# A 64-expert layer on one core: two of four batches as 127 tiles of expert-sorted rows, between two dense parts

## The chip, the cores and the metric
The kernel runs on one core of a Trainium2 chip. The metric is the device time of one execution in microseconds, the median over several runs. TensorE is PE here, its weight loads PEld, VectorE DVE, ScalarE ACT, GpSimd POOL, SyncE SP.

## The reference
A decoder of four rounds over x of 4 batches x 512 tokens x 128 features: each round has an attention, a cross attention and a feed-forward part, each added to x. The change is in the feed-forward part of the third round, a mixture of 64 experts with 8 chosen per token. In short, with h the layernorm of x:
```
logits = h @ gate_w.T                        # 64 per token
p      = softmax(logits); w = top 8 of p, divided by their sum
x     += sum over the 8 of w[e] * (silu(h @ w_gate[e].T) * (h @ w_up[e].T)) @ w_down[e].T
```
`w_gate` and `w_up` are 64 x 96 x 128, `w_down` is 64 x 128 x 96. Everything is float32.

## The kernel before, in words
The program is a row of stages. Each stage is a block in which every engine runs its own list in program order and waits on semaphores that are written out by hand, and a stage ends when all engines are through. x, y and a are resident tensors of 128 features x 2048 tokens; `k.big` holds a layer's weights, loaded by SP well ahead; `k.ps` are the eight PSUM banks of 512 columns. `layer8` (L1764) is the 64-expert layer.

It computes all 64 experts for all tokens. The 64 x 96 hidden features are cut into J = 48 blocks of 128, and a unit is one block for one batch of 512 tokens: units go over pairs of batches, blocks, and the two batches of a pair, 192 in all. A unit is nine matmuls of 128x512 by `three` (L770), which makes a float32 product of three fp32r ones, with the weights split in `wh` + `wl` and the data in `yh` + `yl`: three for the gate, three for up, and, LAG = 3 units later, three for the down product, which add up in `sums` over the 48 blocks. ACT takes the silu of the gate (L1934), DVE (even units, L2023) or POOL (odd ones, L1840) multiplies it by the routing weights, DVE multiplies by up (L2001), ACT copies the result to `hh` (L1940) and DVE takes the rest `hl` (L2006). POOL splits the weights of a block (L1829, L1831). The routing weights come as `rep`: 128 hidden features x 1024 tokens, in which each row repeats its expert's weight. SP reads them in two or three pieces per block from `routing` in DRAM (L1820), into a ring of R = 3.

Before the first unit, DVE finds the top 8 of batches 0 and 1 with `max` and `match_replace`, norms, transposes and stores the weights; those of batches 2 and 3 follow in 12 steps between units (`route`, L1992 is `finish`).

The 8-expert layer of the first round, `layer2` (L778), already works on sorted rows, and rows of it are among those below. There POOL scatters token rows of 512 bytes to the places of their expert in DRAM by indirect DMAs of 128 rows (L906), SP reads back four tiles at a time (L869) and fetches the experts' weights (L861), PE turns the tiles (L938) and multiplies with the expert's columns addressed from registers that it loads in `address`, twice in all (L948, L952, L965), DVE copies results out (L1144), SP stores them (L874), POOL gathers them back (L828) and DVE mixes them with their shares (L844, L846). The places in DRAM are cleared before, by POOL at the start of the program (L169). `l0_lookup_mlp` (L318) is the second half of the first stage's layer, with its last matmuls at L353 and its last add at L424.

## Time and profile before
| | |
|---|---|
| median of 3 runs | 2006.56 us (2006.14 to 2015.05) |
| the profiled execution, its own time | 1991.04 us |
| its span, first to last instruction | 1989.2 us |
| mean granted TensorE clock over the span | 0.938 |
| busy: PE, PEld, DVE, ACT, POOL | 1764.9, 1270.9, 1239.4, 1058.3, 830.7 us |
| DMA: bytes, mean | 131.88 MB, 66 GB/s |

Busy time is that in which an engine worked on an instruction; a matmul's includes its way through the array, so matmuls that follow each other overlap. A line of the page and of the trace names the line of the code, the engine, the operation and the tensors (out<-in, without buffer numbers). "idle before" is the time for which the engine stood still ahead of the group, with what ended it. The clock is a fraction of 2.4 GHz.

### The profile page before, as it was taken

How to read it: one execution, taken by the hardware profiler on the slowest of the kernel's cores; microseconds unless marked ns; L12 is line 12 of the kernel's file. 1: busy time of each engine (PE TensorE's matmuls, PEld its weight loads, DVE VectorE, ACT ScalarE, POOL GpSimd, SP SyncE). 2: the span in 40 equal slices, each digit the busy share in tenths (PEclk: the TensorE clock that was granted, in tenths of full speed). 3: DMA queues.
4: the chain of work that ended last, by engine and by line, in shares of the span. 5: the costliest groups of instructions: out<-in, count | busy, mean ns of one | idle time of the engine just before them, and what ended most of it. 6: DMA issues, size and time to landing. Idle time of an engine off the chain costs nothing. (4 is left out here: it accounts for less than half of the span.)

```text
span 1989.2 us, 50832 instructions
## 1 busy us (share of the span) xinstructions
PE 1764.9 (89%) x20095; PEld 1270.9 (64%) x20114; DVE 1239.4 (62%) x2436; ACT 1058.3 (53%) x2386; POOL 830.7 (42%) x1085
## 2 busy tenths in 40 slices
PE   7883998756899999999998779999999999999886
PEld 4332997334568888888887537888788756633332
DVE  4544444477667777777853437888888768634434
ACT  4551444557776666666644345555555541166552
POOL 1004231124457767676652006666666610044201
PEclk9996999977899999999997889999999989699998
DMA  7002784000230000000000405444444300000100
GB/s 282 1 1 77 216 255 138 14 1 0 74 108 15 24 14 25 14 24 14 17 22 24 191 6 147 129 130 130 127 128 128 106 1 1 1 2 1 39 1 22
DMA packets 51182, 131.88 MB, mean 66 GB/s; under 512 B 11288, under 2 KB 23200, under 8 KB 50048
## 3 DMA queue, kind: packets, MB, share of 16 engines
q1 hardware_dynamic: 47040, 121.24, 19.4%
q0 software_dynamic: 2816, 7.21, 1.1%
q8 instruction: 164, 2.69, 0.6%
q14 instruction: 74, 0.61, 0.1%
q10 hardware_dynamic: 1088, 0.13, 0.0%
HBM read 110.47 MB, written 18.09 MB: 65 GB/s over the span
## 5 line engine op out<-in xcount | busy, mean ns | idle before, releaser
L2558 DVE SCALAR_TENSOR_TENSOR big<-bank,pack,big 128x256 f32<-128x256 f32 (+2 forms) x384 | 182.9, 477 | 39.3 <-ACT mask L2447 23.5
L2006 DVE TENSOR_TENSOR hl<-bank,hh 128x512 fp32r<-128x512 f32 x192 | 132.8, 692 | 65.2 <-ACT hh L1940 55.6
L1940 ACT ACTIVATE hh<-bank 128x512 fp32r<-128x512 f32 x192 | 115.1, 599 | 86.0 <-DVE bank L2001 84.5
L2446 ACT ACTIVATE big<-bank,pack 128x256 f32<-128x256 f32 x192 | 91.5, 477 | 129.0 <-PE bank L2254 124.7
L773 PE MATMUL bank<-yh,wl 128*128 128x512 f32 x384 | 151.6, 395 | 5.4 <-DVE yl L1950 2.5
L774 PE MATMUL bank<-yl,wh 128*128 128x512 f32 x384 | 150.5, 392 | 0.0
L775 PE MATMUL bank<-yh,wh 128*128 128x512 f32 x384 | 150.4, 392 | 0.0
L1840 POOL TENSOR_TENSOR a<-a,rep 128x512 f32<-128x512 f32 x96 | 125.5, 1307 | 30.4 <-DMA rep<-routing 25.7
L2001 DVE TENSOR_TENSOR bank<-bank,a 128x512 f32<-128x512 f32 x192 | 133.2, 694 | 7.0 <-PE bank L775 0.9
L2958 ACT ACTIVATE pt<-bank 128x1024 f32<-128x1024 f32 (+3 forms) x128 | 79.5, 705 | 99.1 <-PE bank L2810 99.0
L2164 POOL TENSOR_TENSOR big<-big,mask 128x256 f32<-128x256 f32 (+1 forms) x128 | 93.8, 732 | 88.8 <-DVE big L2558 56.4
L2740 POOL TENSOR_SCALAR_AFFINE_SELECT pt<-pt 128x256 f32<-128x256 f32 x128 | 55.0, 442 | 175.3 <-ACT pt L2958 173.0
L2254 PE MATMUL bank<-y,pack 128*128 128x262 f32 (+1 forms) x384 | 120.8, 400 | 4.2 <-DVE big L2558 4.0
L2241 PE MATMUL bank<-big 128*128 128x128 f32 x896 | 123.2, 284 | 1.4 <-issue 1.4
L1829 POOL CAST wh<-big 128x384 fp32r<-128x384 f32 x96 | 48.8, 508 | 167.9 <-PE bank L775 114.2
L2241 PEld LDWEIGHTS bank<-big 128*128 128x128 f32 x896 | 107.1, 191 | 6.6 <-issue 3.0
L2984 DVE TENSOR_REDUCE part<-bank 128x8 f32<-128x1024 f32 (+1 forms) x80 | 93.8, 1218 | 24.5 <-PE bank L2790 23.8
L1139 DVE SCALAR_TENSOR_TENSOR a<-bank,big,a 128x128 f32<-128x128 f32 x184 | 51.8, 344 | 83.5 <-ACT a L1051 83.4
L1831 POOL TENSOR_TENSOR wl<-big,wh 128x384 fp32r<-128x384 f32 x96 | 98.7, 1028 | 7.7
L2790 PE MATMUL bank<-big 32*128 32x128 f32 (+1 forms) x1024 | 92.6, 355 | 4.2 <-DVE part L2984 4.2
L2790 PEld LDWEIGHTS bank<-big 32*128 32x128 f32 x1024 | 74.3, 222 | 33.0 <-issue 18.8
L773 PEld LDWEIGHTS bank<-yh,wl 128*128 128x128 f32 x384 | 72.5, 189 | 29.4 <-issue 4.8
(601 smaller groups left out, 4504.8 us busy)
## 6 DMA issues: line engine op xcount, KB each, us to landing
rep<-routing SPq DMA_DIRECT2D x64, 384.0 KB, 3.5
big<-in_experts SPq DMA_DIRECT2D x46, 516.0 KB, 3.8
rep<-routing SPq DMA_DIRECT2D x64, 256.0 KB, 4.0
big<-in_big SPq DMA_DIRECT2D x1, 9216.0 KB, 26.3
gate<-big SPq DMA_DIRECT2D x32, 256.0 KB, 2.0
z<-gate SPq DMA_DIRECT2D x16, 512.0 KB
rep<-routing SPq DMA_DIRECT2D x64, 128.0 KB, 3.7
pack<-in_pack SPq DMA_DIRECT2D x1, 5846.5 KB, 21.1
```

The source lines that it names most:

```text
L773: nc.tensor.matmul(out, pl, dh[:, cur], start=start, stop=False)
L774: nc.tensor.matmul(out, ph, dl[:, cur], start=False, stop=False)
L775: return nc.tensor.matmul(out, ph, dh[:, cur], start=False, stop=stop)
L1831: nc.gpsimd.tensor_tensor(low, src, high.bitcast(F32), ALU.subtract).then_inc(s["w_low"], 1)
L1840: nc.gpsimd.tensor_tensor(spread_(m), spread_(m), spread(n), ALU.mult).then_inc(s["odd"], 1)
L1940: nc.scalar.activation(hh[:, sl((n - 1) % 3)], up_bank(n - 1), ACT.Copy).then_inc(s["high"], 1)
L2001: nc.vector.tensor_tensor(up_bank(n), up_bank(n), other, ALU.mult).then_inc(s["h"], 1)
L2006: nc.vector.tensor_tensor(hl[:, sl(n % 3)], up_bank(n), hh[:, sl(n % 3)].bitcast(F32), ALU.subtract).then_inc(s["low"], 1)
L2241: mm4 = lambda out, gr, left_, right: [nc.tensor.matmul(out[:, sl(h % GH, P)], left_(h), right(h), start=True, stop=True) for h in hs(gr)][-1]
L2254: nc.tensor.matmul(haloed(i)[:, :, 3 - halo:], k.w["L2_attn_qkv_w"][:, sl(m, P)], tokens, start=True, stop=True).then_inc(s["raw"], 1)
L2558: ins = nc.vector.scalar_tensor_tensor(out=d, in0=conv_in(i, back), scalar=weight(i, 3 - back), in1=d, op0=ALU.mult, op1=ALU.add)
L2790: mm = nc.tensor.matmul(both(at)[:, gl * S + c * w:][:, 0:w], qj[b][rows, j * S + i * P:][:, 0:P], kd[b][rows, key:key + w], start=kind != ...
```

## The change
Batches 2 and 3 stay dense, batches 0 and 1 become rows sorted by expert. The layer's list on PE is: blocks 0 to 25 of batches 2 and 3 (52 units), then 127 tiles of 128 rows (8 x 1024 rows and up to 127 rows of padding for each of 64 experts, rounded down), two to a step, then blocks 26 to 47 (44 units).

- In a dense unit gate and up are still three fp32r matmuls each; the down product is one matmul of float32, `h` is no longer split, LAG is 2 and the silu goes to SBUF (`sg`). POOL multiplies and splits weights only for the first five blocks, then DVE multiplies for all units and takes `wl`, ACT makes `wh`. Blocks now cover 4 experts x 32 features, three blocks share a `rep` row set, and SP loads a quarter per expert (4 DMAs per 3 blocks).
- In the first part DVE also ranks the picks of batches 0 and 1 (a scan), finds each row's place (`locate`, `situate`), and for each of the 8 picks writes 8 columns of places (`put`). POOL then issues 64 indirect DMAs (L1901 of the changed kernel) that scatter the rows to `wide_rows`.
- In the tile part SP reads four tiles per DMA and stores the results two tiles at a time, from two places in `out`. PE transposes four tiles at a time (L1969) and then computes, two tiles at a step, gate and up together as one matmul of 192 columns (L1981), a transpose of `h` (L1989), the down matmul (L1996). Every 8 steps it loads 32 addresses into registers (L1974). ACT does `lay`, silu, `tile_lay`; DVE the product and `evict`.
- In the second dense part POOL issues 64 indirect DMAs that gather the results (L1907), 8 per 128 tokens, into two halves of `found`, and DVE mixes 8 rows with their shares after units 60, 64, 69, 73, 78, 82, 87 and 91. PE turns the sums back (`join`) and DVE adds them to x.
- SP clears the 127 tiles' rows in DRAM with six DMAs at the end of `l0_lookup_mlp` (L340 of the changed kernel), and the 8-expert layer's SP waits for them before its first fetch. A second copy of the down weights, 96 x 8192, is loaded in the first dense part (`wide_down`).

```diff
+WIDE_TILES = (2 * S * 8 + 64 * (P - 1)) // P
+WIDE_SPLIT, WIDE_POOLED, WIDE_PLACE_AT, WIDE_MAP_AT = 26, 5, 8, 15
+WIDE_MIX_AT = [2 * WIDE_SPLIT + 8 + 9 * i // 2 for i in range(8)]
...
+        @block.sync
+        def _(sp):
+            sp.wait_ge(s["down"], B)
+            for lo in range(0, WIDE_TILES, SORTED):
+                n = min(SORTED, WIDE_TILES - lo)
+                sp.dma_start(k.wide_rows[lo * P:(lo + n) * P, :].rearrange("(n p) d -> p n d", p=P), k.big[:, 0:n * D].rearrange("p (n d) -> p n d", d=D)).then_inc(k.wide_cleared, 16)
...
+            sp.wait_ge(k.wide_cleared, 16 * -(-WIDE_TILES // SORTED))
...
+        sg, h = (lambda n: k.past[:, sl(n % 2)]), (lambda n: a[:, sl(n % 3)])
...
+            def bring_rows(q):
+                after(sp, s["turned"], q - 2)
+                n = min(4, WIDE_TILES - 4 * q)
+                src = rows_in[4 * q * P:(4 * q + n) * P, :].rearrange("(n p) d -> p n d", p=P)
+                sp.dma_start(rows[:, q % 3 * S:][:, 0:n * P].rearrange("p (n d) -> p n d", d=D), src).then_inc(s[f"x_{q % 3}"], 16)
+
+            def store(p):
+                n = len(tiles(p))
+                sp.wait_ge(s["evicted"], p + 1)
+                dst = rows_out[2 * p * P:(2 * p + n) * P, :].rearrange("(n p) d -> p n d", p=P)
+                sp.dma_start(dst, out[:, p % 2 * 2 * P:][:, 0:n * P].rearrange("p (n d) -> p n d", d=D)).then_inc(s[f"stored_{p % 2}"], 16)
...
+            sp.wait_ge(s["scattered"], 16 * K8 * HALF)
+            bring_rows(0)
+            bring_rows(1)
+            for p in range(PAIRS):
+                if p % 2 == 0 and p // 2 + 2 < turns:
+                    bring_rows(p // 2 + 2)
+                store(p)
+            for q in range(before, G // 4):
+                bring_rep(q)
...
+            for m in range(WIDE_POOLED):
                 n = 2 * m + 1
...
-                nc.gpsimd.tensor_tensor(spread_(m), spread_(m), spread(n), ALU.mult).then_inc(s["odd"], 1)
-                if m + 2 < N // 2:
...
+                nc.gpsimd.tensor_tensor(sg(n), sg(n), spread(n), ALU.mult).then_inc(s["odd"], 1)
...
+            for c in range(K8):
+                pool.wait_ge(s["placed"], c + 1)
+                for i in range(HALF):
+                    nc.gpsimd.indirect_dma_start(out=rows_in, out_offset=bass.IndirectOffsetOnAxis(where[:, c * HALF + i:][:, 0:1], 0), in_=y[:, sl(i, P)], in_offset=None).then_inc(s["scattered"], 16)
+            for half in range(2):
+                pool.wait_ge(s[f"stored_{half}"], 16 * len(range(half, PAIRS, 2)))
+            for i in range(HALF):
+                after(pool, s["mixed"], i - 1)
+                for c in range(K8):
+                    nc.gpsimd.indirect_dma_start(out=found[:, sl(i % 2 * K8 + c, P)], out_offset=None, in_=rows_out, in_offset=bass.IndirectOffsetOnAxis(where[:, c * HALF + i:][:, 0:1], 0)).then_inc(s[f"got_{i % 2}"], 16)
...
+            def unit(n):
+                m, b = n // 2, n % 2
...
+                pe.wait_ge(s["y_low"], b + 1)
+                after(pe, s["silu"], n - 1)
+                three(nc, gate_bank(n), (part(wh, m, 0), part(wl, m, 0)), (yh, yl), sl(b), True, True).then_inc(s["gate"], 1)
+                after(pe, s["h"], n - 1)
+                three(nc, up_bank(n), (part(wh, m, 1), part(wl, m, 1)), (yh, yl), sl(b), True, True).then_inc(s["up"], 1)
+
+            def down(n):
+                pe.wait_ge(s["h"], n + 1)
+                nc.tensor.matmul(sums(n), down_block(n // 2), h(n), start=n < 2, stop=n >= N - 2).then_inc(s["down"], 1)
+
+            def turn(q):
+                after(pe, s["laid"], q)
+                pe.wait_ge(s[f"x_{q % 3}"], 16 * (q // 3 + 1))
+                for n in range(min(4, WIDE_TILES - 4 * q)):
+                    mm = nc.tensor.transpose(turn_bank[:, sl(n, P)], rows[:, q % 3 * S + n * P:][:, 0:P], k.ident)
+                mm.then_inc(s["turned"], 1)
...
+            def address(c):
+                held = [pe.alloc_register(f"column_{c}_{i}_{nc.next_id()}") for i in range(32)]
+                pe.load(held, first_col[0:1, sl(c, 32)])
...
+            def tile_gu(p):
+                pe.wait_ge(s["laid"], p // 2 + 1)
+                after(pe, s["tile_h"], p - 1)
+                for i, n in enumerate(tiles(p)):
+                    mm = nc.tensor.matmul(gu_bank(p)[:, sl(i, 2 * F)].rearrange("p (w f) -> p w f", w=2), xt[:, n // 4 % 2 * S + n % 4 * P:][:, 0:P],
+                                          gate_up_cols[:, :, bass.ds(columns[n][0], F)], start=True, stop=True)
+                mm.then_inc(s["tile_gu"], 1)
+
+            def tile_flip(p):
+                pe.wait_ge(s["tile_h"], p + 1)
+                after(pe, s["tile_ht"], p)
+                for i, n in enumerate(tiles(p)):
+                    mm = nc.tensor.transpose(flip_bank[0:F, sl(i, P)], tile_h(p)[:, sl(i, F)], k.ident)
+                mm.then_inc(s["flipped"], 1)
+
+            def tile_down(p):
+                pe.wait_ge(s["tile_ht"], p + 1)
+                after(pe, s["evicted"], p - 1)
+                for i, n in enumerate(tiles(p)):
+                    mm = nc.tensor.matmul(down_bank(p)[:, sl(i, P)], tile_ht(p)[:, sl(i, P)], wd[0:F, bass.ds(columns[n][1], P)], start=True, stop=True)
+                mm.then_inc(s["tile_down"], 1)
...
+            for p in range(PAIRS + 2):
+                if p % 2 and p // 2 + 1 < turns:
+                    turn(p // 2 + 1)
+                if p < PAIRS:
+                    if p % 8 == 0:
+                        address(p // 8)
+                    tile_gu(p)
+                if 0 < p <= PAIRS:
+                    tile_flip(p - 1)
+                if p > 1:
+                    tile_down(p - 2)
...
-                    three(nc, gate_bank(n), (part(wh, n, 0), part(wl, n, 0)), (yh, yl), sl(units[n][2]), True, True).then_inc(s["gate"], 1)
-                    after(pe, s["low"], n - 2)
-                    three(nc, up_bank(n), (part(wh, n, 1), part(wl, n, 1)), (yh, yl), sl(units[n][2]), True, True).then_inc(s["up"], 1)
...
-                    three(nc, sums(b), (part(wh, m, 2), part(wl, m, 2)), (hh, hl), sl(m % 3), j == 0, j == J - 1).then_inc(s["down"], 1)
...
+            def scale(n):
+                dve.wait_ge(s["silu"], n + 1)
...
+                nc.vector.tensor_tensor(sg(n), sg(n), spread(n), ALU.mult).then_inc(s["odd" if n % 2 else "even"], 1)
...
-                nc.vector.tensor_tensor(up_bank(n), up_bank(n), other, ALU.mult).then_inc(s["h"], 1)
...
-                nc.vector.tensor_tensor(hl[:, sl(n % 3)], up_bank(n), hh[:, sl(n % 3)].bitcast(F32), ALU.subtract).then_inc(s["low"], 1)
+                nc.vector.tensor_tensor(h(n), up_bank(n), sg(n), ALU.mult).then_inc(s["h"], 1)
...
+            def dense(m):
+                scale(2 * m)
+                hidden(2 * m)
+                if m >= WIDE_POOLED:
+                    scale(2 * m + 1)
+                if WIDE_POOLED <= m + 2 < J:
+                    split_low(m + 2)
+                if 2 * m in WIDE_MIX_AT:
+                    mix(WIDE_MIX_AT.index(2 * m))
+                hidden(2 * m + 1)
+                if 2 * m + 1 in WIDE_MIX_AT:
+                    mix(WIDE_MIX_AT.index(2 * m + 1))
...
+            def evict(p):
+                n = len(tiles(p)) * P
+                dve.wait_ge(s["tile_down"], p + 1)
+                after(dve, s[f"stored_{p % 2}"], 16 * (p // 2))
+                nc.vector.tensor_copy(out[:, p % 2 * 2 * P:][:, 0:n], down_bank(p)[:, 0:n]).then_inc(s["evicted"], 1)
+
+            def mix(i):
+                cur = o[:, sl(i, P)]
+                dve.wait_ge(s[f"got_{i % 2}"], 16 * K8 * (i // 2 + 1))
+                for c in range(K8):
+                    row, part_of = found[:, sl(i % 2 * K8 + c, P)], share[:, c * HALF + i:][:, 0:1]
+                    if c == 0:
+                        ins = nc.vector.tensor_scalar(cur, row, part_of, None, ALU.mult)
+                    else:
+                        ins = nc.vector.scalar_tensor_tensor(out=cur, in0=row, scalar=part_of, in1=cur, op0=ALU.mult, op1=ALU.add)
+                    if c < K8 - 1:
+                        link(ins)
+                ins.then_inc(s["mixed"], 1)
...
+            def pick(dst, c, values):
+                link(nc.vector.scalar_tensor_tensor(out=tmp, in0=rank, scalar=float(c + 1), in1=values, op0=ALU.is_equal, op1=ALU.mult))
+                link(nc.vector.tensor_reduce(dst[:, sl(c, HALF)], tile(tmp), AX.X, ALU.add))
+
+            def put(c):
+                pick(spot, c, at)
+                nc.vector.tensor_copy(where[:, sl(c, HALF)], spot[:, sl(c, HALF)]).then_inc(s["placed"], 1)
...
```

PE's list within the first dense part, before: two gates and ups with a down product (`hh`, `hl`) between them, nine rows for three rows each of gate, up and down.
```order
L773 MATMUL bank<-yh,wl 128x512
L774 MATMUL bank<-yl,wh 128x512
L775 MATMUL bank<-yh,wh 128x512
L773 MATMUL bank<-yh,wl 128x512
L774 MATMUL bank<-yl,wh 128x512
L775 MATMUL bank<-yh,wh 128x512
L773 MATMUL bank<-hh,wl 128x512
L774 MATMUL bank<-hl,wh 128x512
L775 MATMUL bank<-hh,wh 128x512
```
And in the changed kernel at the same place (`three` is at L783 to L785 there, the down product at L1963):
```order
L783 MATMUL bank<-yh,wl 128x512
L784 MATMUL bank<-yl,wh 128x512
L785 MATMUL bank<-yh,wh 128x512
L783 MATMUL bank<-yh,wl 128x512
L784 MATMUL bank<-yl,wh 128x512
L785 MATMUL bank<-yh,wh 128x512
L1963 MATMUL bank<-a,big 128x512
```
Three rows of `hh` and `hl` have become one of `a` and `big`; six of `yh` and `yl` stay.

PE's list in the tile part of the changed kernel, across a load of addresses; ISA rows are register arithmetic, L1996 the down matmuls, L1989 the transposes of `h`, L1981 gate and up:
```order
L1996 ISA
L1996 MATMUL bank<-wd,a 128x128
L1996 ISA
L1996 MATMUL bank<-wd,a 128x128
L1974 TENSOR_LOAD first_col
L1975 ISA x4
L1981 ISA
L1981 MATMUL bank<-big,pack 128x192
L1981 ISA
L1981 MATMUL bank<-big,pack 128x192
L1989 MATMUL bank<-pack,a 96x128 x2
L1996 ISA
```
None of these rows is in the list before; each matmul with an expert's weights has a register row of its own.

POOL's list at the end of its multiplications, before (the pattern goes on for all 96 blocks of the two pairs):
```order
L1840 TENSOR_TENSOR a<-a,rep 128x512
L1829 CAST wh<-big 128x384
L1831 TENSOR_TENSOR wl<-big,wh 128x384
L1840 TENSOR_TENSOR a<-a,rep 128x512
L1829 CAST wh<-big 128x384
L1831 TENSOR_TENSOR wl<-big,wh 128x384
```
and in the changed kernel, where it ends after five blocks:
```order
L1875 TENSOR_TENSOR wl<-big,wh 128x256
L1893 TENSOR_TENSOR pack<-pack 128x512
L1873 CAST wh<-big 128x256
L1875 TENSOR_TENSOR wl<-big,wh 128x256
L1893 TENSOR_TENSOR pack<-pack 128x512 x2
L1901 DMA wide_sorted<-y,where 16256x128 x64
L1907 DMA pack<-results,where 128x128 x64
```
The passes over `a` and `wl` are gone from there on, and 128 indirect DMAs stand in their place.

## Rows read from the trace of the kernel before
**Rows 1.** Windows: busy us (count) of PE, PEld, DVE, ACT, POOL; clock; DMA share; GB/s
```profile
235.00:260.00 25.00, 25.00 (x227) 24.91 (x226) 11.71 (x45) 11.68 (x38) 0.00 (x0) 1.00 0.77 224
340.00:361.00 21.00, 16.92 (x50) 7.21 (x48) 11.07 (x20) 13.21 (x20) 15.29 (x16) 1.00 0.19 50
1400.00:1500.00 100.00, 100.00 (x441) 81.41 (x440) 79.53 (x123) 57.26 (x97) 66.99 (x73) 1.00 0.42 127
```
**Rows 2.** Group by form, 1196 to 1600: busy us, mean ns, idle before
```profile
L2006 DVE TENSOR_TENSOR hl<-bank,hh 128x512 fp32r<-128x512 f32 x192 | 132.8, 692 | 65.2 <-ACT hh L1940 55.6 <-DVE pack L1976 1.4 <-DVE top L1972 0.4
```
**Rows 3.** Timeline, edges of the 64-expert layer: start, us, engine, line
```profile
1190.16 0.76 PE L773 MATMUL bank<-yh,wl 128*128 128x512 f32 x1 [2.46 <-DVE yl L1950]
...
1197.55 0.69 DVE L2023 TENSOR_TENSOR a<-bank,rep 128x512 f32<-128x512 f32 x1 [5.61 <-DMA rep<-routing]
...
1593.41 0.69 DVE L1992 TENSOR_TENSOR x<-x,bank 128x512 f32<-128x512 f32 x1 [1.06 <-PE bank L775]
```
**Rows 4.** Timeline, PE, two fp32 matmuls of 128x512
```profile
1172.49 1.02 PE L1852 MATMUL bank<-rep,pack 128*128 128x512 f32 x2
1173.35 1.02 PE L1847 MATMUL bank<-x,pack 128*128 128x512 f32 x2
```
**Rows 5.** Timeline, POOL, an indirect DMA of the 8-expert layer
```profile
188.75 0.97 POOL L906 DMA_INDIRECT sorted<-y,where  x1 [0.30 <-issue]
```
**Rows 6.** Timeline, a POOL pass beside a DVE pass of two SBUF inputs
```profile
1300.13 1.30 POOL L1840 TENSOR_TENSOR a<-a,rep 128x512 f32<-128x512 f32 x1
...
1304.11 0.72 DVE L1986 TENSOR_TENSOR pack<-pack,mx 128x512 f32<-128x512 f32 x1
1304.23 1.76 POOL L1840 TENSOR_TENSOR a<-a,rep 128x512 f32<-128x512 f32 x1
```
**Rows 7.** Timeline, indirect DMAs beside four such DVE passes
```profile
174.06 0.69 DVE L1072 TENSOR_TENSOR gt<-lg 128x512 f32<-128x512 f32 x1
174.37 1.22 POOL L906 DMA_INDIRECT sorted<-y,where  x1 [0.30 <-issue]
...
175.90 1.02 POOL L906 DMA_INDIRECT sorted<-y,where  x1 [0.30 <-issue]
176.12 0.69 DVE L1075 TENSOR_TENSOR gt<-gt,eq 128x512 f32<-128x512 f32 x1
```
**Rows 8.** DMA issues of the whole run: KB each, us from issue to landing
```profile
sorted<-big POOLq DMA_DIRECT2D x2, 1472.0 KB, 19.5
results<-out SPq DMA_DIRECT2D x46, 64.0 KB, 2.5
big<-sorted SPq DMA_DIRECT2D x10, 256.0 KB, 4.5
...
sorted<-y,where POOLq DMA_INDIRECT x32, 2.6
```
**Rows 9.** Timeline, PE in the 8-expert loop: four transposes, two times four matmuls
```profile
226.42 0.60 PE L938 MATMUL bank<-pack,big 128*128 128x128 f32 x4
226.85 1.06 PE L948 MATMUL bank<-xt,big 128*128 128x128 f32 x8
227.75 1.06 PE L952 MATMUL bank<-xt,big 128*128 128x128 f32 x8
```
**Rows 10.** Timeline, PE after the register load of the 8-expert loop
```profile
211.63 0.57 PE L948 MATMUL bank<-xt,big 128*128 128x128 f32 x3 [1.42 <-issue]
```
**Rows 11.** Groups by form of the 8-expert loop, small shapes
```profile
L1144 DVE COPY out<-bank 128x128 f32<-128x128 f32 x46 | 12.9, 280 | 1.1 <-PE bank L965 1.1
...
L1026 ACT ACTIVATE xt<-bank 128x256 f32<-128x256 f32 x1 | 0.4, 384 | 0.8 <-PE bank L938 0.8
```
**Rows 12.** Timeline, DVE, a mix of the 8-expert layer
```profile
306.25 0.28 DVE L844 TENSOR_SCALAR o<-big,share 128x128 f32<-128x128 f32 x1
306.57 0.35 DVE L846 SCALAR_TENSOR_TENSOR o<-big,share,o 128x128 f32<-128x128 f32 x1
```
**Rows 13.** Timeline, SP, the first expert fetches
```profile
172.68 2.71 SPq L861 DMA_DIRECT2D big<-in_experts  x3
```

509 lines of the change are left out of this document (331 added, 178 removed).

## The prediction
> **What bounds the kernel now.** I read the slices first, where TensorE is full all through the 64-expert layer, then windows inside it: over 100 us PE is busy for 100.00 with 441 matmuls, DVE 79.5, ACT 57, POOL 67, clock 1.00, DMA share 0.42 [rows 1]. The groups by form show what fills the other engines: besides the product of `h`, a DVE pass (L2006) and an ACT copy (L1940) per unit that only split `h` in two, 192 times; the DVE pass waits mostly for ACT, which costs nothing as PE is full [rows 2]. So inside the layer TensorE's own work sets the pace and only its beginning is a wait. The timeline gives the edges: first dense matmul 1190.1, first `rep` row used 1197.55, last add ends 1594.1 [rows 3]. The dense part is thus 404.0 us, and 192 units x 9 matmuls x 0.227 us (100 us by 441) is 392.
>
> The sum is made against the profiled execution, 1991.04 us with a span of 1989.2; the median of the runs shown is 2006.56, 15.5 us above it. I take the same difference off both.
>
> **The dense parts.** 96 units are left of 192. A unit keeps six fp32r matmuls, 6 x 0.227 = 1.36 us, and its three down matmuls become one in plain fp32. Two such 128x512 matmuls start 0.86 us apart [rows 4] (each is two records), so the down product costs 0.86 instead of 0.68 and a unit 2.22 instead of 2.04 us. The hand-over: PE can do three and a half units' gates and ups (3.5 us of its work) before it needs the first `h`, and that needs `rep`, as now at 1197.55, then two DVE passes of 0.69: 1199.0, which is 8.9 us after 1190.1. Then 52 x 2.22 - 3.5 = 111.9, and `place` adds eight small bf16 products and eight of 64 columns, at the fp32r price per column 1.6: PE is through part one at 122.4 (all from 1190.1).
> DVE in part one has per pair of units two scales, two products and a split of 256 columns, about 3.1 us, plus a `put` of 1.45 each second pair (a 512 pass, a 512 reduce, a cast), against 4.45 of PE: covered. The routing of batches 0 and 1 lies in the same gap. If that cover went, the next thing late would be `h`.
>
> **The scatters.** The first `put` comes after unit 11, 8.9 + 21.5 (12 units less the 3.4 done and two downs) + 1.6 = 32.0, plus 0.7 and 1.45: 34.2. From there POOL issues 64 indirect DMAs. In the 8-expert layer they take 0.97 and 0.30 between two, 1.27 us [rows 5]. But DVE's new `scale` reads two SBUF tensors, where the old one read PSUM and SBUF. A POOL pass that met such a DVE pass took 1.76 instead of 1.30 us [rows 6]: 0.46 lost for 0.72. Against this, two indirect DMAs issued across four such DVE passes in a row (2.75 us) took 1.22 and 1.02 instead of 0.97 [rows 7]: 0.30 lost for 2.75, or 0.11 per us. These are the ends, 0.11 and 0.64; I take 0.11, since it is measured on the very instruction. DVE is in such passes for 0.45 of the time (two scales of 0.65 and a split of 0.37 in 4.45 us, and a 0.69 pass of a `put` in 8.9), so an indirect costs 1.27 / (1 - 0.11 x 0.45) = 1.335: 64 make 85.4, done at 119.6. Landing 2.6, then the first four tiles read back in 4.5 [rows 8]: 126.7. So PE waits 4.3 us here.
> The Trainium skill, "GPSIMD Engine Reference", section 1 (Specifications), says that GpSimd's SBUF interface is shared with VectorE and contends with DVE instructions of two SBUF inputs, and "SBUF — State Buffer", section on the two separate sides, that descriptors of a POOL-issued DMA can't be written while DVE holds the port; taken as full exclusion, the gap would be 1.27 / 0.55 = 2.3 us per DMA and part one 60 us longer. By that rule, [rows 6] agree for a plain POOL pass, [rows 7] show far less for indirect DMAs.
>
> **The tiles.** 127 are computed whatever the routing needs. A 128-column fp32 matmul costs 0.222 us (four between two starts in [rows 9], 0.89), a transpose, which is one record and not two, 0.108 (four in 0.43); 192 columns at the matmul's rate 0.33. A tile has one transpose in, gate and up together (192), one transpose of `h`, one down: 0.108 x 2 + 0.33 + 0.222 = 0.768, a pair 1.54. That is short enough for a second bound to stand level with it, the two places of `out`: evict 0.41, landing 2.5 from the issue [rows 8], hand-overs 0.2, so 3.1 us for two pairs, 1.55 each. Two bounds that tie jitter: I take 1.62, and 63.5 pairs make 102.9 us. The register loads: each eight pairs PE loads 32 columns; the one such load inside the 8-expert loop cost PE 1.42 us of standing still [rows 10], and 7 x 1.42 = 9.9. First turn, first `lay`, filling and draining the chain: 5. Eight `pick`s of 1.4 us stand before an evict and make its store late by as much: 1 us each, 8. Together 125.8, so to 252.5.
> What must hide under it: ACT's silu, lay of 96x256 and half a 512 lay, about 0.4 + 0.38 + 0.3; DVE's product and evict, 0.36 + 0.41 (from [rows 11], and from the 0.69 of a 512 pass); DMA, 512 rows of 512 bytes, at 31 ns a row on 16 engines (0.19 x 21 us x 16 / 2048 rows, the gather window of [rows 1]) 1.0. From a pair's gate and up to its transpose PE has 1.3 us of other pairs' work, and silu and product with three hand-overs of 0.1 need 1.1.
>
> **The second dense part.** 44 units, 97.7 us. The gathers: POOL is held up again, with DVE in two-SBUF passes for 0.62 of the time (0.37 as before, and seven of 0.35 per `mix`), 1.36 us each; the last of 64 is issued at 4 + 87 after the part's start, landed at 93.7. A `mix` is eight chained passes, 0.32 + 7 x 0.39 = 3.05 us [rows 12]. With it DVE has 7.0 + 3.05 per 4.5 units and PE 10.0, so DVE is as full as PE and every mix delays `h` by 0.4 to 1.2 us: 8 x 0.8 = 6.4. The last mix ends at 96.7, four units, join and adds follow: 105.5, by PE's own count 97.7 + 6.4 + 1.6, the same. The layer's part ends at 358.0 in place of 404.0: 46.0 us less.
>
> **The rest.** SP now clears 127 tiles at the end of the lookup MLP: six issues at 0.45, half of what three expert fetches took each with their register loads, 2.71 / 3 [rows 13], while that stage's last add takes 0.7: +2, ends 0 and +5. The bytes, 8.3 MB, run beside the next layer: two clears of 1.47 MB landed in 19.5 us beside other loads, so 60 us at worst [rows 8], and SP issues its first fetch only at 172.7 [rows 13], 68 us after the last product of that stage: nothing. If that cover were gone the fetch of experts would be late by what is missing. `wide_down`, 3.1 MB, loads beside part one: nothing. 128 fewer `rep` issues on SP: nothing, SP is not waited for.
> Sum: -46.0 + 2 = -44.0, **1947.0 in profile terms and 2006.6 - 44.0 = 1962.6 us**. From about 10 us on (0.5%) a measurement of this kernel tells a change from none.
>
> **Rivals.**
> *A. POOL starves (slower).* Mechanism: DVE's two-SBUF passes keep POOL from writing descriptors, on POOL's queue at L1901 and L1907. At 0.64 lost per us (the other end above) a scatter costs 1.79, +29 us before the tiles; a gather 2.1, so part two is 152 instead of 105.5: +47. -44 + 76 = +32, 2039 us. It turns the sign from a loss of about 0.45 per us on. For: the trace's POOL pass; the scheme keeps both parts just long enough. Against: the indirect rows. 0.10. The rule of the Trainium skill's "SBUF — State Buffer" named above, taken as total exclusion, goes past this end: +62 before the tiles, and gathers of 3.3 us; [rows 7] don't bear it out.
> *B. The tile chain is latency (slower).* The two-place `out` sets the pair instead of PE. If a result lands as late as the read-back does, 4.5 us [rows 8], two pairs take 5.1, a pair 2.55: 63.5 x 0.93 = +59, +15 in all, 2022 us. The sign turns at 1.62 + 44 / 63.5 = 2.31 us a pair. For: each pair crosses PE four times, and DVE does the evict in line with the product of a later pair. Against: landing 2.5 was under full weight traffic (0.77 of the DMA engines), and the 8-expert loop, built alike, has no gap in 227 matmuls [rows 1]. 0.07.
> *C. Part of the gain.* Pairs near 1.9 (+18) and indirects near 1.5 (+14), or the clears at 1.6 an issue (+7) in the place of a part of it: -12, 1995 us. 0.21.
> *D. It doesn't wait where I say:* pairs at 1.54, no stall at mixes or picks: -44 - 5 - 6 - 8, 1944 us. 0.12. That the tiles are fewer than said is no case: 127 is fixed in the loop.
> *Forecast:* 0.50, with 1952 to 1976 as its own range.
>
> **How the numbers follow.** Faster by over 0.5%: forecast, D and two thirds of C, 0.76; within: the rest of C and the near ends of A and B, 0.10; slower: A and B, 0.14. The range leaves out A and B above, and the outer part of D below: 1945 to 2000.
>
> **What would show it.** Right: a unit of the dense parts at 2.2 us; L1981 and L1996 starts giving 1.6 us per pair with gaps of about 1.4 at L1974; L1901 and L1907 1.27 to 1.4 apart; PE's wait before the first L1969 under 6 us; a few waits on DVE's `h` near the mixes. Wrong: indirect DMAs 1.7 us apart or more with PE idle on x_0 or DVE idle on got_0 (A); evict waiting for results<-out, or L1989 for DVE, in each pair (B); a TensorE clock below full in the tiles, which I don't expect since the 8-expert loop shows 1.00; SP's L340 issues over 1 us each.

## The result, and the profile after

The changed kernel takes 2109.85 us (median of 4 runs, 2099.49 to 2134.65); the kernel before, run beside it, 2010.8 (median of 4 runs). The ratio is 1.0461, 95% interval 1.0366 to 1.0555, and it leaves out the run of 2134.65 us, which is over 1.5% above the fastest and counts as slow. So the kernel is slower by 3.7 to 5.6%, where the prediction had 1962.6 us, faster, and a range that ended at 2000. The profiled execution took 2099.49 us (span 2097.8, clock 0.913) against the 1991.04 on which the prediction's sum was made: +108.5.

Where these 108 us lie, from the first DVE instruction of one stage to the first of the next, in us:

| | before | after | |
|---|---|---|---|
| start of the 8-expert layer | 161.1 | 169.2 | +8.1 |
| 8-expert layer | 180.5 | 212.1 | +31.6 |
| 64-expert layer | 421.2 | 508.8 | +87.6 |
| causal attention behind it | 281.1 | 263.6 | -17.5 |
| the rest | | | -1.3 |

And inside the 64-expert layer, by the prediction's own edges (from the first dense matmul, 1229.68; a turn is the transposing of four tiles, L1969):

| | forecast | after |
|---|---|---|
| to the first tile turn | 126.7 | 158.8 |
| tiles | 125.8 | 211.1 |
| second dense part | 105.5 | 122.1 |
| sum | 358.0 | 492.0 |

The windows of the changed kernel (columns as in [rows 1]): a quiet piece of part one, part one with the scatters, the tiles, part two.

```profile
1243.00:1270.00 27.00, 26.66 (x105) 17.68 (x104) 22.44 (x53) 8.28 (x16) 7.26 (x8) 0.97 0.51 112
1270.00:1388.00 118.00, 98.45 (x312) 60.95 (x311) 70.23 (x126) 28.32 (x58) 64.60 (x64) 0.90 0.22 71
1388.00:1600.00 212.00, 139.76 (x767) 127.92 (x766) 59.72 (x147) 60.00 (x160) 0.00 (x0) 0.82 0.27 74
1600.00:1721.00 121.00, 107.87 (x367) 68.80 (x365) 88.86 (x178) 32.14 (x64) 64.63 (x64) 0.96 0.23 64
```

As long as POOL issues no DMA, PE is full. From the first scatter on it is not, though no other engine is: DVE 70 of 118 us, ACT 28. In the tiles PE has 140 of 212, and the mean granted clock falls to 0.82: it changes between its two levels, 1.2 and 2.4 GHz. A kernel that lost its bound to another engine would show one that is full; this one shows waits.

The unit itself is as forecast. Two down products of neighbouring units in PE's timeline, which answer to [rows 4]:

```profile
1250.09 1.02 PE L1963 MATMUL bank<-a,big 128*128 128x512 f32 x2
...
1252.33 1.02 PE L1963 MATMUL bank<-a,big 128*128 128x512 f32 x2
```

2.24 us apart, forecast 2.22. The waits while POOL scatters (engine, line, what it waited for: us in total, times, longest):

```profile
ACT pack L2089 <- remote: 39.3, 7, 9.2
...
POOL wide_sorted L1901 <- DVE where L2220: 19.2, 3, 8.9
...
DVE pack L2236 <- issue: 15.9, 6, 4.9
PE bank L783 <- issue: 12.0, 6, 3.3
```

"issue" and "remote" are waits for which the profile finds no releaser. They come together on three engines, in bouts, as I call such a stretch from here on. One of them in the timeline:

```profile
1317.42 1.02 PE L1963 MATMUL bank<-a,big 128*128 128x512 f32 x2
...
1318.69 0.96 POOL L1901 DMA_INDIRECT wide_sorted<-y,where  x1 [0.30 <-issue]
1319.66 0.60 ACT L2089 ACTIVATE pack<-bank 128x512 f32<-128x512 f32 x1 [6.62 <-remote]
...
1320.29 0.69 DVE L2236 TENSOR_TENSOR pack<-pack 128x512 f32<-128x512 f32 x1 [4.90 <-issue]
1320.40 0.47 PE L783 MATMUL bank<-yh,wl 128*128 128x512 f32 x1 [1.97 <-issue]
...
1324.67 0.80 PE L783 MATMUL bank<-yh,wl 128*128 128x512 f32 x1 [3.34 <-issue]
...
1332.89 1.16 POOL L1901 DMA_INDIRECT wide_sorted<-y,where  x1 [6.92 <-DVE where L2220]
```

PE, ACT and DVE come to a few instructions between long waits, while POOL goes on at its even 1.26 us per DMA. In the end DVE's next list of rows is late, POOL has to wait for it, and a few us after POOL stops the others run again. Such bouts begin at about 1285, 1318, 1354, 1620 and 1653, each inside a stretch of indexed DMAs.

The tiles have another wait:

```profile
DVE a L2267 <- ACT a L2103: 138.0, 62, 5.3
...
PE bank L1969 <- DMA pack<-wide_sorted: 59.1, 27, 3.0
...
PE bank L1981 <- issue: 13.1, 8, 2.1
```

The 138 us of DVE are the largest number and the least telling: DVE waits for ACT, ACT for PE, and PE (second line) for the rows of its next turn, 27 times. The third line is the register load ahead of each 16 tiles. The low clock is a cost of its own: two transposes of L1969 start 0.109 us apart where the granted clock is 1.00 and 0.214 where it is 0.50. SP and PE around one turn:

```profile
1443.80 0.47 SPq L1841 DMA_DIRECT2D pack<-wide_sorted  x1
1444.71 5.16 SPq L1847 DMA_DIRECT2D results<-pack  x2
...
1447.08 0.63 PE L1969 MATMUL bank<-pack 128*128 128x128 f32 x4 [2.86 <-DMA pack<-wide_sorted]
```

The rows needed at 1444.2 were asked for at 1443.80. The clears, and what DMAs took from issue to landing (answers to [rows 8]):

```profile
85.24 25.05 SPq L340 DMA_DIRECT2D wide_sorted<-big  x6
```
```profile
results<-pack SPq DMA_DIRECT2D x63, 128.0 KB, 1.9
pack<-wide_sorted SPq DMA_DIRECT2D x31, 256.0 KB, 3.1
wide_sorted<-big SPq DMA_DIRECT2D x5, 1472.0 KB, 13.4
```

### The profile page after: what moved, and what is told of

Its sections match the earlier page's. It is cut to its first block and busy times, and to the rows that moved or that the text cites. A ratio compares the mean times of both kernels' runs of the same rounds, so it can differ in the third digit from the quotient of the medians.

```text
span 2097.8 us, 50146 instructions
## 1 busy us (share of the span) xinstructions
PE 1753.5 (84%) x19958; PEld 1233.6 (59%) x19958; DVE 1160.7 (55%) x2428; ACT 960.4 (46%) x2302; POOL 704.7 (34%) x947
## 3 DMA queue, kind: packets, MB, share of 16 engines
q0 software_dynamic: 6912, 15.61, 2.4%
## 5 line engine op out<-in xcount | busy, mean ns | idle before, releaser
L1907 POOL DMA_INDIRECT pack<-results,where x64 | 64.6, 1010 | 271.5 <-DMA results<-pack 239.3
L2089 ACT ACTIVATE pack<-bank 128x512 f32<-128x512 f32 x96 | 57.3, 599 | 197.5 <-PE bank L785 111.2
L783 PE MATMUL bank<-yh,wl 128*128 128x512 f32 x192 | 115.9, 604 | 36.6 <-issue 17.2
L1963 PE MATMUL bank<-a,big 128*128 128x512 f32 x192 | 104.0, 628 | 0.0
L2236 DVE TENSOR_TENSOR pack<-pack 128x512 f32<-128x512 f32 x91 | 63.0, 692 | 70.1 <-issue 31.1
L2267 DVE TENSOR_TENSOR a<-bank,a 128x192 f32<-128x192 f32 x64 | 22.8, 355 | 142.0 <-ACT a L2103 138.0
L3291 DVE TENSOR_REDUCE part<-bank 128x8 f32<-128x1024 f32 (+1 forms) x80 | 93.5, 1216 | 8.2 <-PE bank L3097 7.3
L1062 ACT ACTIVATE a<-bank,big 128x128 f32<-128x128 f32 x184 | 52.2, 369 | 83.3 <-PE bank L959 56.7
L783 PEld LDWEIGHTS bank<-yh,wl 128*128 128x128 f32 x192 | 38.5, 200 | 78.3 <-issue 53.7
L838 POOL DMA_INDIRECT big<-results,where x32 | 30.9, 965 | 146.7 <-DMA results<-out 72.4
L1981 PE MATMUL bank<-big,pack 128*128 x254 | 68.7, 404 | 13.1 <-issue 13.1
```

The lines of the kernel that those rows point to most:

```text
L783: nc.tensor.matmul(out, pl, dh[:, cur], start=start, stop=False)
L1907: nc.gpsimd.indirect_dma_start(out=found[:, sl(i % 2 * K8 + c, P)], out_offset=None, in_=rows_out, in_offset=bass.IndirectOffsetOnAxis(whe ...
L1963: nc.tensor.matmul(sums(n), down_block(n // 2), h(n), start=n < 2, stop=n >= N - 2).then_inc(s["down"], 1)
L1981: mm = nc.tensor.matmul(gu_bank(p)[:, sl(i, 2 * F)].rearrange("p (w f) -> p w f", w=2), xt[:, n // 4 % 2 * S + n % 4 * P:][:, 0:P], gate_u ...
L3291: nc.vector.tensor_reduce(dst, src, AX.X, ALU.max).then_inc(s["most"], 1)
```

## The experiments

Times of parts are counted as in the tables above. The first four change one thing each in the changed kernel.

### Clears in neighbouring rows

```diff
-rearrange("(n p) d -> p n d", p=P), k.big[:, 0:n * D].rearrange("p (n d) -> p n d", d=D))
+rearrange("(p n) d -> p (n d)", p=P), k.big[:, 0:n * D])
```

> One edit to the changed kernel: in the clears every partition writes whole neighbouring rows (23 rows of 512 bytes that lie together) instead of 23 rows that lie 128 rows apart. The six clears took SP 25.05 us to issue (393 to 5253 ns each) from 85.24 on, and the next stage began 5.2 us later than before, ended 7.0 and started the 8-expert layer 8.1 us later. Theory C1, the number of pieces sets the issue time: six issues of under 0.6 us each, the next stage starts within 1 us of the kernel before (105.9), and the 8-expert layer starts 6 to 8 us earlier than in the changed kernel. Rival C2, the bytes in flight delay the stage (8.3 MB at some 290 GB/s take until 110): issues short, but the gap before the 8-expert layer shrinks by less than 3 us. The two bouts of unexplained waits in the 8-expert layer (213.7 to 224, 299.2 to 317.8) are untouched if they come from the scatters and gathers beside them, and gone if they come from the clears.

```profile
82.85 5.64 SPq L340 DMA_DIRECT2D wide_sorted<-big  x6
```

25.05 us of issuing become 5.64 (0.94 apart, not the 0.6 expected), the next stage starts at 103.3 in place of 111.1 and the 8-expert layer at 158.5, not 169.2, both earlier than C1 had it; 2.4 us of either arose before the clears, which begin at 82.85 and not at 85.24. C1 holds: the pieces (23 of 512 bytes per partition, or one of 11.8 KB) set the issue time. Not a microsecond of it shows in the whole: 2112.05 us, ratio 1.0519 (1.0463 to 1.0576). In the profiled execution the bouts further on were longer: part one of the 64-expert layer took 162.6 us (158.8 before the edit), part two 132.3 (122.1), the whole layer 522.8. That the other runs lost it in the same place is not shown. The 8-expert layer kept its bouts (217.7 us), so the clears' issues don't make them.

### No indexed DMAs in the 64-expert layer

```diff
-nc.gpsimd.indirect_dma_start(out=rows_in, ...)
...
-nc.gpsimd.indirect_dma_start(out=found[...], ...)
...
-sp.wait_ge(s["scattered"], 16 * K8 * HALF)
+sp.wait_ge(s["placed"], K8)
...
-dve.wait_ge(s[f"got_{i % 2}"], 16 * K8 * (i // 2 + 1))
```

> The changed kernel with the 64 scatters and 64 gathers of the 64-expert layer left out (tiles read the cleared rows, the mixes read what stands in the buffer; all other work stays). Theory S: the indirect DMAs of POOL hold back the instructions of PE, DVE and ACT (unexplained waits in five bouts, about 12 us each, between 1282 and 1371 and between 1620 and 1702). Then part one runs at 2.22 us per unit throughout, from the first dense matmul to its last in 122 to 124 us, the waits called issue and remote are under 3 us in each dense part, and part two takes 98 to 106 us. Rival P, PE waits for data (h, rep or split weights that DVE can't finish with the new work): the bouts stay and part one takes over 140 us. In both the tile part stays at about 210 us, since its waits are for the read-back. The 8-expert layer is untouched by the edit: if its two bouts are there again at the same places they belong to this program, if not they are a matter of the execution.

2070.62 us, ratio 1.0316 (1.0259 to 1.0374). Its windows, from the piece that had the scatters on:

```profile
1276.00:1364.00 88.00, 88.00 (x313) 58.04 (x312) 69.91 (x126) 28.51 (x57) 0.00 (x0) 1.00 0.17 47
1364.00:1572.00 208.00, 132.23 (x766) 120.99 (x765) 59.12 (x147) 59.46 (x160) 0.00 (x0) 0.86 0.27 75
1572.00:1680.00 108.00, 102.80 (x369) 67.33 (x368) 88.67 (x180) 32.70 (x65) 0.30 (x1) 1.00 0.12 33
```

The same 126 DVE instructions now lie in 88 us instead of 118, and PE is full. From the first dense matmul to the last gate or up product (called the last product of a unit here) part one takes 125.6 us, to the first turn 128.6; part two takes 107.9. Both are up to 2 us above the ranges expected. PE's unexplained waits in both are 0. Theory S holds: without these DMAs there are no bouts. And rival P (PE waits for data of an overloaded DVE) falls: DVE has all its work still. Whether it is the indexed form, the queue or the bytes, this run can't tell; the runs with plain DMAs below ask that. The tiles stay at 207.5, so their trouble is another.

### Rows asked for one turn earlier

```diff
 bring_rows(1)
+bring_rows(2)
 for p in range(PAIRS):
-    if p % 2 == 0 and p // 2 + 2 < turns:
-        bring_rows(p // 2 + 2)
+    if p % 2 == 0 and p // 2 + 3 < turns:
+        bring_rows(p // 2 + 3)
```

> One edit to the changed kernel: SP asks for the rows of a turn of four tiles one turn earlier (three turns before the loop, then turn p/2+3 in place of p/2+2; the ring of three stays). Theory R: the tile part takes 211 us instead of the 126 forecast because SP's request stands behind the store of the pair before, so that it goes out about 3 us before its rows are needed and lands 3.1 us after it: PE waits 59.1 us for wide_sorted in 27 waits, and the low clock that the idling brings (0.83) adds more. Then those waits fall under 10 us in all, the clock in the tile part rises over 0.93, the tile part takes 125 to 150 us and the kernel 2030 to 2055 us. Rival L, the chain from gates through silu, product and turn back sets the pace (3.3 us per pair whatever the rows do): the waits move to ACT and DVE tiles and the part takes over 190 us.

2036.7 us, ratio 1.0066 (1.0023 to 1.0109): 73 us less, by the medians, for the place of one call. The tile window, and all that PE waits for in it:

```profile
1401.00:1527.00 126.00, 108.35 (x767) 102.68 (x766) 58.32 (x147) 57.91 (x160) 0.00 (x0) 0.95 0.45 125
```
```profile
PE bank L1982 <- issue: 17.6, 8, 2.3
```

125.1 us for 211.1: theory R, in full. PE's wait for rows is gone, no other wait of PE has taken its place in this window, and the clock is 0.95. What is left are the eight register loads. The 86 us are the 59.1 that PE waited and 31.4 that the same 767 matmuls are busy less (108.35 for 139.76), as more of them run at the full clock, less 4.5 by which the register loads cost more. The kernel gained less than 86, because the bouts of this execution were longer: part two took 135.9 us, not 122.1.

### POOL pauses after each eight

```diff
             for i in range(HALF):
                 nc.gpsimd.indirect_dma_start(out=rows_in, ...).then_inc(s["scattered"], 16)
+            pool.wait_ge(s["scattered"], 16 * HALF * (c + 1))
...
             for c in range(K8):
                 nc.gpsimd.indirect_dma_start(out=found[...], ...).then_inc(s[f"got_{i % 2}"], 16)
+            pool.wait_ge(s[f"got_{i % 2}"], 16 * K8 * (i // 2 + 1))
```

> One edit to the changed kernel: POOL waits after each eight scatters, and after each eight gathers, until they have landed, before it issues the next. In the profile of the changed kernel each bout of unexplained waits of PE, DVE and ACT begins inside a stretch of 12 or more indirect DMAs and ends 1 to 3 us after POOL pauses. Theory S: a bout can last no longer than the rest of one stretch of eight (10.2 us) and its landing (2.6), so the bouts shrink to about half; the scatters end some 8 x 3 us later less what the bouts give back. Part one and two together give back 10 to 25 us of bouts, and the wait of the tiles for the scatters grows by about as much: the kernel is within 15 us of the changed one. Rival P, the bouts are PE's and DVE's own affair: they keep their length, and the kernel is slower by 15 to 25 us by the later scatters.

```profile
1291.19 0.95 POOL L1901 DMA_INDIRECT wide_sorted<-y,where  x1 [0.30 <-issue]
1293.68 0.96 POOL L1901 DMA_INDIRECT wide_sorted<-y,where  x1 [1.53 <-DMA wide_sorted<-y,where]
```

At a pause POOL stands still for 1.53 us in place of 0.30. The last scatter goes out 133.6 us after the first dense matmul, as before the edit (133.5), since POOL no longer waits for a DVE that is held up: 0.6 us in place of 10.3. PE's last product of a unit is at 126.4 in place of 155.8, first turn at 139.0, part two 113.2. In all 2090.76 us, ratio 1.0401 (1.0322 to 1.048). Theory S again, and better than I had expected: the bouts all but vanish, where I had them at half, and the kernel is 19 us under the changed one, where I had said within 15.

### The kernel before, with the clears alone

```diff
+k.wide_rows, k.wide_cleared = nc.dram_tensor("wide_sorted", (WIDE_TILES * P, D), F32).ap(), nc.alloc_semaphore("wide_cleared")
+sp.dma_start(k.wide_rows[lo * P:(lo + n) * P, :].rearrange("(p n) d -> p (n d)", p=P), k.big[:, 0:n * D]).then_inc(k.wide_cleared, 16)
```

> The kernel before, with one part of the change added: the tensor wide_sorted and its six clears (in the form in which every partition writes neighbouring rows), and SP's wait for them ahead of the 8-expert layer. The 64-expert layer is the one of before. In the changed kernel and all four experiments on it the 8-expert layer takes 212 to 218 us (DVE's first to the next stage's first) with 5 to 16 us of PE waits called issue, against 180.5 and 1.4 in the kernel before, though its code is the same. Theory H, the tensor in memory or its clearing does it: this kernel's 8-expert layer takes 210 to 218 us and the kernel 2040 to 2055 us. Rival N, something else of the new program does (where its instructions lie, or its other tensors): the 8-expert layer takes 178 to 184 us, and this kernel is within 0.5% of the kernel before. By C1 the issues cost nothing either way.

2008.02 us, ratio 0.9983 (0.9952 to 1.0014), and yet an 8-expert layer of 212.2 us with both bouts. The layer is as H had it and the kernel's time as N had it: neither holds as written. The way out is that the profile of before is the odd one, which the next run tested.

### The kernel before, profiled again

> The kernel before, unchanged, profiled once more. Its profiled execution took 1991.04 us while its runs beside ours lie between 2000.5 and 2026.2 with a median near 2015; the kernel before with the clears alone ran as fast as it (0.9983), and yet its profile shows the two bouts of PE waits in the 8-expert layer (212.2 us for the layer), which the profile of before lacks (180.5). Theory E: the bouts come with most executions of the kernel before too, and its one profile was without them. Then this profile shows a layer of 205 to 218 us and a time of 2005 to 2026 us. Rival N, they belong to the new program: 178 to 184 us for the layer, and whatever makes the time over 2000 us lies elsewhere.

2013.04 us. The 8-expert layer in this profile, and in the one that the prediction was made from:

```profile
158.00:370.00 212.00, 159.17 (x1267) 150.64 (x1266) 88.54 (x317) 69.58 (x214) 49.28 (x51) 0.84 0.55 160
```
```profile
161.00:342.00 181.00, 146.67 (x1267) 142.24 (x1266) 88.49 (x317) 68.88 (x214) 48.31 (x50) 0.91 0.63 187
```

The same instructions (1267 matmuls, 317 on DVE) take 211.3 us here and 180.5 there. Theory E holds: the bouts belong to most executions of either kernel. Of the 14 profiles of this study 12 have them in this layer (205 us and more); two, the first of before and that of the last experiment below, have not.

### The kernel before, with pauses

```diff
                     for i in range(2):
                         nc.gpsimd.indirect_dma_start(out=rows_in[g], ...)
+                    if t % 4 == 3:
+                        pool.wait_ge(s[f"scattered_{g}"], 32 * (t - bs[0] + 1))
...
+            pool.wait_ge(late.s[f"got_{b}"], 16 * 2 * TB)
```

> The kernel before with one edit: in the 8-expert layer POOL waits after each eight scatters and each eight gathers until they have landed. In the version with all edits this took the layer from 215.6 to 209.0 us and the kernel from 1998.2 to 1989.8 us. Theory S: the same here, 5 to 12 us less than the kernel before (ratio 0.994 to 0.9975), so that of the 1% by which the version with all edits beats the kernel before, at least half is the change of the 64-expert layer. If the ratio is under 0.992, most of that 1% is the pauses' own.

2008.91 us, ratio 0.998 (0.9946 to 1.0014), 8-expert layer 207.4. No difference that can be told from none. In that layer PE is still held back inside the stretches of eight, and the layer is only 4 us shorter than in the second profile of before, one execution against one. Why pauses help the 64-expert layer and hardly this one is open.

### Three edits together, and four

The changed kernel with the first, third and fourth edit:

> The changed kernel with the three edits of the first experiments together: clears of neighbouring rows, rows asked for one turn earlier, POOL's pauses after each eight indirect DMAs of the 64-expert layer. Against the changed kernel they gave in their layers 5 to 10 us at the beginning (start of the 8-expert layer 158.5 for 169.2), 86 us in the tile part (125.1 for 211.1), and 20 us in part one (139.0 for 158.8) with 9 in part two (113.2 for 122.1). If they add up, the 64-expert layer takes 389 to 400 us (421.2 in the kernel before, 508.8 in the changed one), part one 139, tiles 125, part two 113, and the kernel 1985 to 2010 us. If the pauses only moved the waits, part one or two is back over 150 or 120.

1998.17 us, ratio 0.9931 (0.9903 to 0.996): 141.3 + 129.0 + 113.4 us. The gains add up. With the pauses in the 8-expert layer as well:

> The three edits, and the same pauses in the 8-expert layer: POOL waits after each eight scatters and after each eight gathers until they have landed. Theory S says of that layer what it says of the other: PE's bouts there (10 and 18 us, inside stretches of 32 scatters and 16 gathers) shrink to what is left of a stretch of eight, so the layer takes 180 to 192 us instead of 212 to 218, and the kernel 1955 to 1985 us, under the kernel before. Rival Q: the bouts of the 8-expert layer have another cause than the long stretches (its refills fall at the same places as in the kernel before, which had the stretches and no bouts): the layer stays over 205 us and this kernel is within 10 us of the one with three edits.

1989.81 us, ratio 0.99 (0.9868 to 0.9933), 8-expert layer 209.0. Theory S had promised 180 to 192 there; that part of it failed, as the run above confirms, and rival Q is nearer. The parts of the 64-expert layer:

```profile
1222.00:1361.00 139.00, 124.66 (x437) 81.32 (x436) 97.08 (x188) 40.97 (x79) 76.19 (x75) 0.94 0.36 96
1361.00:1489.00 128.00, 109.85 (x760) 104.51 (x761) 58.14 (x146) 58.03 (x160) 0.00 (x0) 0.91 0.45 125
1489.00:1604.00 115.00, 104.03 (x372) 67.42 (x370) 88.73 (x178) 32.39 (x64) 64.85 (x64) 1.00 0.25 68
```

381.8 us from the first dense matmul, 404.3 in the kernel before: 22.5 us less, where the forecast was 46.0.

### Four units more ahead of the tiles

```diff
-WIDE_SPLIT, WIDE_POOLED, WIDE_PLACE_AT, WIDE_MAP_AT = 26, 5, 8, 15
+WIDE_SPLIT, WIDE_POOLED, WIDE_PLACE_AT, WIDE_MAP_AT = 28, 5, 8, 15
```

> The version with all edits, and the first dense part two blocks (four units) longer: 56 units ahead of the tiles instead of 52, the places of the mixes moved with it. There PE had finished part one 11.5 us before the first tile (last product of a unit at 1350.0, tiles from 1361.5), since the scatters, which begin 40.6 us after the first dense matmul and take 93, set that time; and part two (114.6 us) is set by the gathers (93.8 us from 4.5 us after the tiles on, then the last mix, the join and the add), not by its 44 units (97.7). If that is so, four units (8.9 us) move into a gap and none of them is missed behind: part one stays at 139 to 141, part two at 112 to 116, and the layer loses... nothing, as both bounds stay: the 64-expert layer takes 396 to 399 us again, within 2 us of 397.8, and PE's idle time moves from before the tiles to part two. If the layer is shorter by over 4 us, PE's own work bound part two; if longer by over 4, the gathers and the units did collide less when there were more units.

1988.56 us, ratio 0.9852 (0.9801 to 0.9902), the fastest against its neighbours. Parts 140.1 + 129.9 + 109.8 = 379.8, 2 us less than with 26: PE's last down product of part one ends at 139.8 and the tiles begin at 140.1, so the gap before them is used up; part two, four units shorter, gave 5 us. The layer took 395.7 us, within the 4 us of 397.8 that the expectation allowed, but part two came under its 112: the gathers did not bind it as firmly as I had said. The medians of the two versions are not apart.

### Plain DMAs in place of indexed ones

```diff
-nc.gpsimd.indirect_dma_start(out=rows_in, out_offset=..., in_=y[:, sl(i, P)], in_offset=None)
+pool.dma_start(rows_in[sl(c * HALF + i, P), :], y[:, sl(i, P)])
-nc.gpsimd.indirect_dma_start(out=found[:, sl(i % 2 * K8 + c, P)], ..., in_=rows_out, in_offset=...)
+pool.dma_start(found[:, sl(i % 2 * K8 + c, P)], rows_out[sl(c * HALF + i, P), :])
```

> The changed kernel with the 64 scatters and 64 gathers of the 64-expert layer replaced by plain DMAs from the same queue of POOL, at the same places and behind the same waits: the same 64 KB each, to and from 128 rows that follow one another in memory (rows are not sorted, and each token gets the rows at its own place). Theory S1, it is POOL's software queue as such that holds PE's instructions back: the bouts stay, part one takes over 145 us from the first dense matmul to the last product of a unit (155.8 in the changed kernel, 125.6 without any of these DMAs) and part two over 115. Rival S2, it is the indexed form (one piece per row, made by POOL from the indices): the bouts are gone, part one takes 124 to 130 us and part two 104 to 112.

2060.03 us, ratio 1.0208 (1.0114 to 1.0303). Part one took 125.4 us to the last product, part two 107.9, no unexplained wait of PE in either, while the 8-expert layer, whose DMAs stayed indexed, had its bouts (211.1 us): S2. The queue moved exactly the packets and bytes it moves in the changed kernel (6912, 15.61 MB). But POOL also had breaks of 4.7 us, so one run more:

```diff
-sp.wait_ge(s["scattered"], 16 * K8 * HALF)
+sp.wait_ge(s["scattered"], 16 * WIDE_TILES)
...
 pool.dma_start(rows_in[sl(c * HALF + i, P), :], y[:, sl(i, P)]).then_inc(s["scattered"], 16)
+if c + i:
+    pool.dma_start(rows_in[sl(63 + c * HALF + i, P), :], y[:, sl(i, P)]).then_inc(s["scattered"], 16)
```

> The kernel with plain DMAs in place of the indexed ones, and in part one a second plain DMA of the same rows behind each (127 in place of 64, the second to the rows of the other tiles). With plain DMAs the bouts were gone (part one 125.4 us from first dense matmul to the last product, no unexplained wait of PE), but POOL also stood still for 4.7 us of every 9, where the indexed form keeps it issuing without a break for 20 to 30 us. Now eight pairs of plain DMAs take POOL 8.5 us of every 8.9. Theory F, the indexed form does it: part one stays at 124 to 130 us and PE's unexplained waits under 3 us, with twice the bytes. Rival K, the unbroken issuing does it: bouts come back, and part one takes over 138 us. Part two, with one plain DMA each, stays at 104 to 112 us either way.

```profile
1261.87 0.54 POOL L1901 DMA_DIRECT2D wide_sorted<-y  x1
1262.40 0.54 POOL L1903 DMA_DIRECT2D wide_sorted<-y  x1
1263.36 0.54 POOL L1901 DMA_DIRECT2D wide_sorted<-y  x1 [0.42 <-DVE where L2222]
```
```profile
1206.00:1334.00 128.00, 123.60 (x434) 81.53 (x433) 96.92 (x187) 40.81 (x79) 77.51 (x138) 0.95 0.49 140
```

POOL issues almost without a break, twice the DMAs, and part one takes 125.8 us to its last product. (2035.33 us, ratio 1.0204, 1.0064 to 1.0343.) That is what theory F expects. But this execution is one of the two in which the 8-expert layer had no bouts either (182.1 us), with indexed DMAs in stretches of 32 and 16. So it may have been spared whatever POOL issued, and it doesn't exclude rival K. What stands is the run before: in one execution the indexed DMAs of one layer came with bouts, and plain ones of the same queue, packets and bytes in the other layer came without. There POOL also paused after each eight, and with such pauses indexed DMAs made hardly any bouts in this layer either. So the queue and the bytes are out; whether the indexed form alone does it or needs the unbroken issuing is not shown.

## Why the prediction was wrong

**The mechanism of the gain was right.** A unit takes 2.24 us for 2.22. An indexed scatter takes 1.30 us for 1.335 (64 in 93.5 us, less 10.3 of waiting for DVE), a gather 1.32 for 1.36. Without indexed DMAs part one is 128.6 for 126.7 and part two 107.9 for 105.5; with the rows at hand the tiles are 125.1 for 125.8. Put together from two runs (it was not run as one kernel) that is 361.6 us for a forecast of 358.0. The measured 492.0 are 134 above the forecast; two things that the sum did not have make 130 of them.

**"The tiles": "a pair 1.54 ... I take 1.62".** It took 3.3. The step costed PE, the places of `out`, ACT, DVE and the DMA engines, and left out SP's own queue: `bring_rows` stands behind the `store` of the pair before, and the ring of three was one turn short of using it. The landing was even better than the 4.5 us of [rows 8], 3.1, and so some 2 us too late each time. This is 86 of the 130 us, shown by moving one call. With the waits came a sign of being wrong that the prediction had named and not expected, a clock below full in the tiles: 0.82, and still 0.95 with the rows at hand. Rival B had the right shape (a pair over 2.31 us turns the sign) and the wrong queue: one evict of the changed kernel waited for a result, 0.6 us. With the rows at hand B's own wait begins to show, nine evicts and 5.2 us in all, and PE did not wait for it. Inside this step a second, small error: the price of a register load came from a load of 23 columns [rows 10], and these are of 32: 2.2 us each on average, 17.6 for the eight in the run with early rows, where the sum had 9.9. Of the 13 us set aside for picks and jitter less than 5 were needed, and that made up for it by luck.

**"The scatters" and "The second dense part".** I asked what DVE does to POOL's DMAs (rival A, and the two rules of the Trainium skill) and never what they do to the others. The scatters' price, and the case against A, held: 1.30 us is far from the 1.79 of A or the 2.3 of full exclusion. The full exclusion was a misreading: the Trainium skill, "SBUF — State Buffer", section on the two separate sides, says that `tensor_tensor` has no 2-port mode and contends, with two SBUF inputs, with what GpSimd reads, and it names only the 2-port modes as keeping it from writing descriptors. By that rule, these runs agree: the passes in question are `tensor_tensor`, and a scatter beside them lost 0.03 us over the 1.27 of [rows 5]. The cost was on PE, in waits that the two steps put at nothing: 30 us in part one and 14 in part two of the profile of the changed kernel, and in the two other versions without pauses 31 to 34 and 24 to 28. The profile I had could not show it: it is one of the two executions of fourteen in which the indexed DMAs of the 8-expert layer made no bout. And the row that I leaned on, "no gap in 227 matmuls", could not show it in any execution: the window 235 to 260 has no instruction of POOL at all [rows 1], and in the second profile of before, with bouts at about 204 and 288, it holds the same 227 matmuls in 25.00 us. There was one sign: the profiled execution lay 15.5 us below the median of the runs, and the prediction carried the difference over as a constant instead of asking what the others had that this one lacked. Against the second profile of before the 8-expert layer is no part of the loss (212.1 and 211.3), and the loss is nearly all in the 64-expert layer: 86.0 of 86.5 us.

**The first scatter** came 41.0 us after the first dense matmul, not 34.2. `h` was ready at 11.0 for 8.9 (before it PE did two and a half units' gates and ups, not the three and a half of the text; the 3.5 us of the sum fit two and a half). The other 4.7 us lie in DVE's list after that, with waits for POOL's product of the odd units (L1893) of 2.07 and 1.54 us among them; no run takes them apart. It matters now: with the pauses the scatters set the end of part one.

**"The rest": "six issues at 0.45 ... +2".** The sign named for it came, "SP's L340 issues over 1 us each": 5.2 us for the large ones. The price was taken from a fetch with one piece per partition [rows 13]; these had 23. Against the run with neighbouring rows the next two stages start 8 and 11 us later, of which 2.4 arose before the clears.

**The attention behind it** is the same code in 281.1 us before and 263.6 after, with the granted clock at 0.90 and 0.96:

```profile
1595.00:1873.00 278.00, 262.31 (x2224) 139.88 (x2238) 160.86 (x165) 115.01 (x183) 63.99 (x146) 0.90 0.00 1
```
```profile
1722.00:1983.00 261.00, 249.29 (x2240) 128.06 (x2238) 159.72 (x164) 115.30 (x183) 64.15 (x146) 0.96 0.00 1
```

This is not the change's doing: with before's layer it took 263.0 in the run with pauses, and 280.1 in the fastest version.

## What to carry to other kernels

Cost a load-ahead by its place in the queue of the engine that issues it: the third place of a ring buys nothing when the request stands behind a store that waits for the result of the tiles before. One profile is one execution: where it lies below the median of its own runs, find what the others have more before pricing anything off it. Before citing a window as free of a cost, see that what would cause it runs in it. And judge indexed DMAs beside compute by the unexplained waits of the other engines, in a run that replaces them by plain ones of the same bytes, and look whether that execution has bouts elsewhere, as a spared one proves nothing.
